# Expert part's first two chunks enter during the last feeding step of an eight-layer linear-attention kernel

## The chip, the cores and the metric

The kernel runs on one core of one Trainium2 chip. The metric is the device time of one execution in microseconds (us), the median over runs. TensorE is called PE here, VectorE DVE, ScalarE ACT, GpSimd POOL, as in the profile. L815 is line 815 of the kernel file.

## The reference, cut to what matters

The input x has 4096 tokens of 128 features. First come eight layers of linear attention with a feed-forward block, each with two layer norms; then a residual layer norm over `x + attention part`; then a mixture of four experts of which each token takes two; then a residual layer norm again.

```python
def _block(x, p):                      # eight times
    Q = elu(x@Wq + bq) + 1; K = elu(x@Wk + bk) + 1; v = x@Wv + bv
    KV = einsum('nsh,nsh->nh', K, v);  Ksum = K.sum(1)
    V = Q * KV / (Q * Ksum + 1e-6)
    x = layernorm(gelu(V@Wo + bo) + x, ln1_s, ln1_b)          # 1e-6
    h = gelu(x@Wf1 + bf1)
    x = layernorm(gelu(h@Wf2 + bf2) + x, ln2_s, ln2_b)
x = _layernorm(x + blocks(x))                                  # 1e-5
h_norm = layer_norm(x, rn_g, rn_b); g = softmax(h_norm @ router_w.T)
top2_w, top2_idx = top_k(g, 2);     top2_w /= top2_w.sum() + 1e-8
hid = relu(layer_norm(einsum('bsd,edh->bseh', x, w1), ln_g, ln_b))
out = sum over the two experts of top2_w * (hid_e @ w2_e)
x = _layernorm(x + layer_norm(out, on_g, on_b))
```

## The kernel before

**Attention part.** The tokens are cut in chunks of 512 columns, features on the partitions. Two chunks (h = 0, 1) are a unit; 4 units times 8 layers make 32 units u = 0 to 31 (`UNITS` = 32). A software pipeline runs over steps s: in step s unit s attends (`attends`), unit s-1 is fed forward (`feeds`), unit s-2 has its second layer norm (`ends`), and s-3 writes the last of it (`closes`). `run` (L321) makes UNITS + 3 steps, so after the last unit has attended in step 31 there come step 32 (unit 31 feeds, unit 30 ends), step 33 (unit 31 ends, the second half of its feed-forward output with it) and step 34 (the last layer norm closes). Each engine has its own list of instructions written out in its own `step` function: the order is by hand, and semaphores tie the lists together. A matrix product in high accuracy is three matmuls (`product`, L681 to L683) on a high and a low part of its operands.

A second layer norm of chunk (u, h) is: `gelu_feed` on ACT (L492), `sum_y`, `high_y`, `low_y` on DVE (L1127, L1134, L1138), `centre` on PE (L799, L800), `square` on ACT (L453), for one half also a cast and a subtraction on DVE (L1145, L1150), `variance` on PE (L818 and L819, or L821), `log_var` and `root` on ACT (L464, L469, as exp(-ln/2)), `normalise` and `high` on DVE (L1160, L1170). GELU and ln/exp need different tables of ACT, loaded by L576 and L619 once each a step.

**Expert part.** Eight chunks. A chunk enters by `add_input` (DVE L1244: last layer's output plus the input x), `turn_z` (PE L867: four transposes so that tokens lie on the partitions), `stats_z` (DVE L1212 to L1232), a power of -1/2 on POOL (`to_minus_half`, L1669), `scale_x` (DVE L1255 to L1264, and POOL L1674), `normalised` (ACT L520, four tiles), `turn_x` (PE L874, back to features on the partitions), `high_x` (ACT L528) and `low_x` (DVE L1270). It is routed by four `gram` products (PE L915 to L917), each followed by `squares` (DVE L1280, four sums), which give the variance of the hidden layer without computing it; then `route` (PE L902 to L904, twelve small matmuls), `gates` (DVE L1316 to L1378), `split_std` (DVE L1291 to L1297), `turn_std` (PE L856) and `rows_of_std` (ACT L507). Then follow `expert_hidden` (PE L888 to L892, eight groups of four) and `expert_out` (PE L925), `mix_tile` (DVE L1392, L1396), and the last norms. A PSUM bank O[0] holds one gram at a time, so a gram waits for the squares of the one before.

`run_moe` (L329) calls the expert steps: in step (0, k) chunk k is routed, chunk k+1 enters, chunk k-1 goes through the experts. Before, chunk 0 enters at the end of step 34 of `run` (the blocks `if s == UNITS + 2`), and the first expert step, `step(0, 0, True, True, False, False)`, routes chunk 0 and lets chunk 1 enter, with no expert work beside it. The table `MIXED`, and `C` and `L` (L173, L325) say which PSUM banks these parts use; `xt_done`, `zt_mm` and `xe_l_done` are the semaphores of `normalised`, `turn_z` and `low_x`.

## Time and profile before

| | |
|---|---|
| median of 3 runs | 1051.41 us (1050.92 to 1051.62) |
| profiled execution | 1052.19 us, its span 1050.1 us |
| mean granted clock of PE | 0.972 |
| busy over the span | PE 961.6 us (92%), DVE 881.4 (84%), ACT 828.6 (79%), POOL 111.5 (11%) |
| instructions | 13399 |

Times in the trace count from the start of the span. The busy time of PE is that of its pipelined matmuls, so a share near 100% is not PE at its peak. The granted clock is a share of PE's 2.4 GHz; 0.50 is 1.2 GHz.

### The profile page before, as it was taken

The page shows a single profiled execution, that of the slowest core. Times are in us where ns is not written, and L with a number is a line of the kernel's source. Part 1 is how long each engine was busy: PE and PEld are TensorE (multiplying, and loading weights), DVE is VectorE, ACT ScalarE, POOL GpSimd, SP SyncE. Part 2 cuts the span into 40 slices and gives each one's busy share as a digit, 9 for nine tenths or more (in the row PEclk, how much of TensorE's full clock was granted, in tenths as well). Part 3 has the DMA queues.
Part 4 walks back from the last instruction along what each step waited for, and adds up shares of the span by engine and source line. Part 5 has one row for each costly group of instructions (what it writes and reads, how often), then busy time and mean ns, then how long its engine had stood idle before and what let it go on. Part 6 is the DMA issues. An engine that isn't in the chain of part 4 may idle for free. (4 is left out here: it accounts for less than half of the span.)

```text
span 1050.1 us, 13399 instructions
## 1 busy us (share of the span) xinstructions
PE 961.6 (92%) x3621; PEld 610.8 (58%) x3621; DVE 881.4 (84%) x2312; ACT 828.6 (79%) x1336; POOL 111.5 (11%) x113
## 2 busy tenths in 40 slices
PE   5799999999999999999999999999998379999993
PEld 3555555555555555655555555555554157877772
DVE  6769999999999999999999999999985457788864
ACT  4689999999999999999899999999987324444452
POOL 3100000000000000000000000000010012323233
PEclk9999999999999999999999999999999669999997
DMA  8000000000000000200000000000020000000000
GB/s 327 1 0 1 1 1 1 0 1 1 1 0 1 1 1 0 81 1 1 1 5 2 1 1 1 1 1 0 1 81 1 0 0 1 12 11 12 11 21 20
DMA packets 8184, 15.86 MB, mean 15 GB/s; under 512 B 944, under 2 KB 5424, under 8 KB 7984
## 3 DMA queue, kind: packets, MB, share of 16 engines
q1 hardware_dynamic: 7680, 14.82, 4.0%
q8 instruction: 31, 0.51, 0.2%
q14 instruction: 41, 0.34, 0.1%
q10 hardware_dynamic: 432, 0.20, 0.1%
HBM read 12.92 MB, written 2.10 MB: 14 GB/s over the span
## 5 line engine op out<-in xcount | busy, mean ns | idle before, releaser
L483 ACT ACTIVATE hid<-R,par 128x512 f32<-128x512 f32 x224 | 148.5, 698 | 15.1 <-PE R L683 13.1
L783 PE MATMUL Oa<-hid,wraw 128*128 128x512 f32 x256 | 133.6, 604 | 1.4
L783 PE MATMUL Ob<-hid,wraw 128*128 128x512 f32 x256 | 130.5, 592 | 0.0
L681 PE MATMUL R<-x_h,wf_h 128*128 128x512 f32 x224 | 105.4, 471 | 0.9 <-ACT hid L483 0.9
L681 PE MATMUL R<-xr_h,wqkv_h 128*128 128x512 f32 x160 | 87.5, 547 | 14.6 <-DVE cen L1512 10.3
L1127 DVE SCALAR_TENSOR_TENSOR y<-x,par,y 128x512 f32<-128x512 f32 x120 | 87.4, 747 | 11.3 <-ACT y L492 11.0
L464 ACT ACTIVATE rs<-SV,eps_ln 128x512 f32<-128x512 f32 x128 | 88.3, 690 | 8.7 <-PE SV L821 6.3
L1138 DVE TENSOR_TENSOR y_l<-y,y_h 128x512 fp32r<-128x512 f32 x128 | 87.8, 686 | 1.2
L682 PE MATMUL R<-x_l,wf_h 128*128 128x512 f32 x224 | 88.0, 393 | 0.0
L683 PE MATMUL R<-x_h,wf_l 128*128 128x512 f32 x224 | 87.9, 392 | 0.0
L469 ACT ACTIVATE rs<-rs 128x512 f32<-128x512 f32 x128 | 80.7, 631 | 1.2
L821 PE MATMUL SV<-y,mean_all 128*128 128x512 f32 x128 | 65.9, 596 | 3.0 <-ACT y L453 2.1
L1114 DVE SCALAR_TENSOR_TENSOR V<-Q,kv,rz 128x512 f32<-128x512 f32 x64 | 46.6, 748 | 24.0 <-ACT rz L448 24.0
L681 PEld LDWEIGHTS R<-x_h,wf_h 128*128 128x128 f32 x224 | 42.0, 187 | 42.0 <-issue 36.0
L783 PEld LDWEIGHTS Oa<-hid,wraw 128*128 128x128 f32 x256 | 45.8, 188 | 35.4 <-ACT hid L483 26.1
L683 PE MATMUL R<-xr_h,wqkv_l 128*128 128x512 f32 x160 | 63.7, 398 | 0.0
L682 PE MATMUL R<-xr_l,wqkv_h 128*128 128x512 f32 x160 | 63.5, 397 | 0.0
L783 PEld LDWEIGHTS Ob<-hid,wraw 128*128 128x128 f32 x256 | 48.3, 189 | 26.2 <-issue 18.2
L681 PEld LDWEIGHTS R<-xr_h,wqkv_h 128*128 128x128 f32 x160 | 30.5, 191 | 54.8 <-DVE xr_l L1183 27.8
L1134 DVE CAST y_h<-y 128x512 fp32r<-128x512 f32 x128 | 54.4, 425 | 9.0 <-PE R L800 6.8
L554 ACT ACTIVATE reluq<-V,rz 128x128 f32<-128x128 f32 x32 | 13.2, 482 | 60.4 <-DVE rz L1411 44.5
L453 ACT ACTIVATE y<-Ca 128x512 f32<-128x512 f32 x64 | 38.0, 595 | 27.3 <-PE Ca L800 27.2
(215 smaller groups left out, 2448.5 us busy)
## 6 DMA issues: line engine op xcount, KB each, us to landing
wraw<-w_dram SPq DMA_DIRECT2D x7, 768.0 KB, 12.1
x<-x_dram SPq DMA_DIRECT2D x8, 256.0 KB, 5.5
Q<-x_dram SPq DMA_DIRECT2D x1, 2048.0 KB, 7.5
out_dram<-reluq SPq DMA_DIRECT2D x8, 256.0 KB, 2.3
wraw<-w_dram SPq DMA_DIRECT2D x2, 512.0 KB, 4.9
wraw<-w_dram SPq DMA_DIRECT2D x1, 576.0 KB, 5.7
wraw<-row_dram SPq DMA_DIRECT2D x1, 512.0 KB, 4.4
wraw<-bias_dram SPq DMA_DIRECT2D x1, 512.0 KB, 5.6
```

The costliest lines, as they stand in the source:

```text
L464: nc.scalar.activation(rs[:, half(h)], SV[:, :], ACT.Ln, bias=eps_ln[:, :]).then_inc(ln_done[which], 1)
L469: nc.scalar.activation(rs[:, half(h)], rs[:, half(h)], ACT.Exp, scale=-0.5).then_inc(rs_done[which], 1)
L483: nc.scalar.activation(hid[:, m * CH:(m + 1) * CH], HIDDEN[m][:, :], GELU, bias=param(u // 4, BF1 + m % FB)).then_inc(hid_done, 1)
L681: nc.tensor.matmul(bank, w_h, a_h, start=True, stop=False)
L682: nc.tensor.matmul(bank, w_h, a_l, start=False, stop=False)
L683: return nc.tensor.matmul(bank, w_l, a_h, start=False, stop=True)
L783: mm = nc.tensor.matmul(O[h][:, :], raw(u // 4, WF2 + j * P, P), hid[:, m * CH:(m + 1) * CH], start=(j == 0), stop=(j == FB - 1))
L821: mm = nc.tensor.matmul(SV[:, :], mean_all[:, :], y[which][:, half(h)], start=True, stop=True)
L1114: nc.vector.scalar_tensor_tensor(out=V[:, half(h)], in0=Q[:, chunk(u, h)], scalar=kv[:, b:b + 1], in1=rz[:, half(h)], op0=ALU.mult, op1=AL ...
L1127: nc.vector.scalar_tensor_tensor(out=g, in0=t, scalar=b, in1=g, op0=ALU.add, op1=ALU.add).then_inc(y_done[which], 1)
L1134: nc.vector.tensor_copy(y_h[:, half(h)], y[which][:, half(h)]).then_inc(yh_done[which], 1)
L1138: nc.vector.tensor_tensor(y_l[:, half(h)], y[which][:, half(h)], y_h[:, half(h)].bitcast(F32), ALU.subtract).then_inc(yl_done[which], 1)
```

## The change

It runs steps 0 to 32 of `run` and drops steps 33 and 34. Into step 32 go: the entering of chunk 0 and of chunk 1 (with `turn_z`, `stats_z`, `scale_x`, `normalised`, `turn_x`, `high_x`, `low_x` of both), and the rest of unit 31's feed-forward output (`feed_out` 4 to 7, `gelu_feed(31, 1)`, `sum_y`, `high_y`, `low_y` of its second half). A new function `last_layer_norms` on each of PE, ACT and DVE takes the place of steps 33 and 34 and of `step(0, 0)`: the last three chunk norms (30, 1), (31, 0), (31, 1) with the four grams and squares of expert chunk 0 between them, then its route, gates and `turn_std`. POOL keeps its `step(0, 0)` as a call of its own. For this the banks of the expert part are exchanged (`C` is CB[1], `L` has CB[0]), the centred values of (31, 1) go to R[1], and some waits name other semaphores.

```diff
-        C, L = CB[0], (SV, CB[1])
+        C, L = CB[1], (SV, CB[0])
...
+        def centred(which, u, h):
+            return R[1] if (which, u, h) == (1, UNITS - 1, 1) else CENTRED[which][h]
...
-            for s in range(UNITS + 3):
+            for s in range(UNITS + 1):
...
         def run_moe(step):
-            step(0, 0, True, True, False, False)
...
+            def last_layer_norms():                     (ACT)
+                u = UNITS - 1
+                nc.scalar.preload_act_table_set("natural_log_exp_and_others")
+                log_var(1, u - 1, 1)
+                root(1, u - 1, 1)
+                square(1, u, 0)
+                square(1, u, 1)
+                log_var(1, u, 0)
+                root(1, u, 0)
+                log_var(1, u, 1)
+                root(1, u, 1)
+                roots_of_hidden(0, 0)
+                exp_logits(0, 0)
+                rows_of_std(0, 0)
...
-                    pe.wait_ge(norm_done[1], 2 * UNITS)     (turn_z, first chunk)
+                    pe.wait_ge(norm_done[0], 2 * UNITS)
...
+                if s == UNITS:                          (PE, step 32, after feed_out 3)
+                    turn_z(0, 1)
                 if ends:
                     variance(1, s - 2, 1)
+                if s == UNITS:
+                    feed_out(s - 1, 4)
+                    feed_out(s - 1, 5)
+                    feed_out(s - 1, 6)
+                    feed_out(s - 1, 7)
+                    turn_x(0, 1)
...
+            def last_layer_norms():                     (PE)
+                u = UNITS - 1
+                gram(0, 0, 0)
+                centre(1, u, 0)
+                gram(0, 0, 1)
+                variance(1, u, 0)
+                centre(1, u, 1)
+                gram(0, 0, 2)
+                variance(1, u, 1)
+                gram(0, 0, 3)
+                route(0, 0)
+                turn_std(0, 0)
...
+            def last_layer_norms():                     (DVE)
+                u = UNITS - 1
+                weave(squares(0, 0, 0))
+                normalise(1, u - 1, 1)
+                high(1, u - 1, 1)
+                weave(squares(0, 0, 1))
+                high_square(1, u, 1)
+                low_square(1, u, 1)
+                weave(squares(0, 0, 2))
+                normalise(1, u, 0)
+                high(1, u, 0)
+                weave(squares(0, 0, 3))
+                normalise(1, u, 1)
+                high(1, u, 1)
+                gating = gates(0, 0)
+                weave(itertools.islice(gating, 7))
+                split_std(0, 0)
+                weave(gating)
```

The words in brackets are mine. How the instructions move is seen at three places. Oa, Ob, Ca, Cb and SV are PSUM banks; every line number is that of the kernel file shown, so the same function has another number in the changed file.

**PE, from the last variance of step 32 on.** Before (L818 to L821 are variances, L783 a feed-forward output, L799 and L800 a centring, L867 `turn_z`):

```order
L818 MATMUL SV<-sq_h,mean_r 128x512
L819 MATMUL SV<-sq_l,mean_r 128x512
L783 MATMUL Ob<-hid,wraw 128x512 x3
L799 MATMUL Ca<-y_h,cen 128x512
L800 MATMUL Ca<-y_l,cen 128x512
L821 MATMUL SV<-y,mean_all 128x512
L783 MATMUL Ob<-hid,wraw 128x512
L799 MATMUL R<-y_h,cen 128x512
L800 MATMUL R<-y_l,cen 128x512
L818 MATMUL SV<-sq_h,mean_r 128x512
L819 MATMUL SV<-sq_l,mean_r 128x512
L867 MATMUL Ca<-consts,y 128x128 x4
```

In the changed kernel (L897 is `turn_z`, L904 `turn_x`, L848, L849 and L851 variances, L813 a feed-forward output, L829 and L830 a centring, L951 to L953 a gram):

```order
L897 MATMUL Cb<-consts,y 128x128 x4
L848 MATMUL SV<-sq_h,mean_r 128x512
L849 MATMUL SV<-sq_l,mean_r 128x512
L813 MATMUL Ob<-hid,wraw 128x512 x4
L904 MATMUL Cb<-consts,x 128x128 x4
L951 MATMUL Oa<-xr_h,x_h 128x512
L952 MATMUL Oa<-xr_h,x_l 128x512
L953 MATMUL Oa<-xr_l,x_h 128x512
L829 MATMUL Ca<-y_h,cen 128x512
L830 MATMUL Ca<-y_l,cen 128x512
L951 MATMUL Oa<-xr_h,x_h 128x512
L952 MATMUL Oa<-xr_h,x_l 128x512
```

The four feed-forward outputs are now in one row, the transposes of chunk 1 stand around them, and the centring of unit 31's first half stands between two grams of chunk 0.

**ACT, from the last GELU of step 32's hidden layer on.** Before (L483 `gelu_hidden`, L492 `gelu_feed`, L464 and L469 the root of the variance, L453 `square`, L520 `normalised`, L528 `high_x`):

```order
L483 ACTIVATE hid<-R,par 128x512
L492 ACTIVATE y<-Oa,par 128x512
L576 ACT_TABLE_LOAD
L464 ACTIVATE rs<-SV,eps_ln 128x512
L469 ACTIVATE rs<-rs 128x512
L453 ACTIVATE y<-Ca 128x512
L464 ACTIVATE rs<-SV,eps_ln 128x512
L469 ACTIVATE rs<-rs 128x512
L619 ACT_TABLE_LOAD
L492 ACTIVATE y<-Ob,par 128x512
L453 ACTIVATE y<-R 128x512
L576 ACT_TABLE_LOAD
```

In the changed kernel, from four GELUs earlier on (L487, L496, L468, L457, L524 and L534 are the same functions):

```order
L487 ACTIVATE hid<-R,par 128x512 x4
L524 ACTIVATE x<-Cb,rz 128x128 x4
L487 ACTIVATE hid<-R,par 128x512 x2
L534 ACTIVATE x_h<-Cb 128x512
L457 ACTIVATE y<-R 128x512
L487 ACTIVATE hid<-R,par 128x512
L496 ACTIVATE y<-Oa,par 128x512
L496 ACTIVATE y<-Ob,par 128x512
L524 ACTIVATE x<-Cb,rz 128x128 x4
L534 ACTIVATE x_h<-Cb 128x512
L669 ACT_TABLE_LOAD
L468 ACTIVATE rs<-SV,eps_ln 128x512
```

Both entries of a chunk (L524, L534) and both `gelu_feed` (L496) now stand under one table. From the first `gelu_feed` on, one table load is left in the layer norms (L669), where there were three (L576, L619, L576).

**DVE in the changed kernel, step 32, behind the statistics of chunk 0.** L1306 is `add_input` of chunk 1, L1189 `sum_y`, L1196 `high_y`, L1222 `normalise`, L1200 `low_y`, and L1317 begins `scale_x` of chunk 0:

```order
L1294 TENSOR_SCALAR rz<-rz 128x4
L1306 TENSOR_TENSOR y<-x,Q 128x512
L1189 SCALAR_TENSOR_TENSOR y<-x,par,y 128x512
L1196 CAST y_h<-y 128x512
L1222 SCALAR_TENSOR_TENSOR x<-Ca,par,rs 128x512
L1200 TENSOR_TENSOR y_l<-y,y_h 128x512
L1317 SCALAR_TENSOR_TENSOR rz<-rz 128x4
L1320 TENSOR_TENSOR rz<-rz 128x4
```

The mean that `normalised` needs (from L1317 on) stands behind four instructions of unit 30's layer norm; before, nothing stood between it and the statistics.

## Rows read from the trace of the kernel before

**Rows 1.** Windows: busy us per engine in a stretch, count in brackets, then PEclk, DMA share, GB/s.

```profile
42.00:44.00 2.00, 2.00 (x5) 1.61 (x6) 1.30 (x2) 1.31 (x3) 0.00 (x0) 0.50 0.03 8
820.00:855.00 35.00, 15.67 (x44) 9.93 (x44) 15.99 (x84) 8.17 (x18) 5.28 (x5) 0.50 0.00 0
855.00:861.00 6.00, 5.94 (x18) 4.59 (x19) 4.27 (x23) 1.36 (x3) 0.00 (x0) 0.50 0.00 0
880.00:1020.00 140.00, 129.64 (x798) 107.91 (x797) 109.87 (x664) 63.70 (x154) 45.89 (x41) 1.00 0.04 11
```

**Rows 2.** PE's timeline, norms to experts: start us, us, instruction, count, [idle before <-releaser].

```profile
815.61 1.02 PE L783 MATMUL Ob<-hid,wraw 128*128 128x512 f32 x2
...
821.72 0.80 PE L799 MATMUL R<-y_h,cen 128*128 128x512 f32 x1 [5.09 <-DVE y_l L1138]
...
829.46 1.11 PE L867 MATMUL Ca<-consts,y 128*128 128x128 f32 x4 [3.35 <-DVE y L1244]
835.45 1.12 PE L874 MATMUL Ca<-consts,x 128*128 128x128 f32 x4 [4.88 <-ACT x L520]
838.07 0.76 PE L915 MATMUL Oa<-xr_h,x_h 128*128 128x512 f32 x1 [1.50 <-DVE x_l L1270]
...
847.49 0.77 PE L915 MATMUL Oa<-xr_h,x_h 128*128 128x512 f32 x1 [1.74 <-DVE Kt L1280]
...
850.23 0.34 PE L902 MATMUL Oa<-rw_h,x_h 128*128 128x4 f32 x1 [1.12 <-DVE Kt L1280]
...
855.06 1.04 PE L856 MATMUL SV<-consts,wraw 128*36 128x128 f32 x4 [1.17 <-DVE wraw L1297]
```

**Rows 3.** ACT's timeline, feeding step 32 to the entry of chunk 0.

```profile
806.93 1.38 ACT L483 ACTIVATE hid<-R,par 128x512 f32<-128x512 f32 x2 [0.88 <-PE R L683]
...
817.18 1.28 ACT L619 ACT_TABLE_LOAD   x1
818.48 0.69 ACT L492 ACTIVATE y<-Ob,par 128x512 f32<-128x512 f32 x1
...
833.89 1.50 ACT L520 ACTIVATE x<-Ca,rz 128x128 f32<-128x128 f32 x4 [6.39 <-DVE rz L1255]
836.60 0.60 ACT L528 ACTIVATE x_h<-Ca 128x512 fp32r<-128x512 f32 x1 [1.21 <-PE Ca L874]
```

**Rows 4.** PE and DVE timelines at full clock: one gram round, route, second `turn_std`.

```profile
868.07 0.47 PE L915 MATMUL Oa<-xr_h,x_h 128*128 128x512 f32 x1 [0.62 <-DVE Kt L1280]
...
869.04 0.29 DVE L1280 SCALAR_TENSOR_TENSOR Kt<-Oa,x 128x128 f32<-128x128 f32 x1 [1.12 <-PE Oa L917]
...
870.12 0.24 PE L902 MATMUL Oa<-rw_h,x_h 128*128 128x4 f32 x1 [0.21 <-DVE Kt L1280]
...
871.45 0.66 PE L874 MATMUL Ca<-consts,x 128*128 128x128 f32 x4
...
873.73 0.61 PE L856 MATMUL SV<-consts,wraw 128*36 128x128 f32 x4
```

**Rows 5.** DVE's timeline of the same norms: `sum_y`, `normalise` and `high`.

```profile
819.19 0.75 DVE L1127 SCALAR_TENSOR_TENSOR y<-x,par,y 128x512 f32<-128x512 f32 x1 [4.04 <-ACT y L492]
...
827.53 0.75 DVE L1160 SCALAR_TENSOR_TENSOR x<-R,par,rs 128x512 f32<-128x512 f32 x1 [2.30 <-ACT rs L469]
828.31 0.49 DVE L1170 TENSOR_SCALAR x<-x,par 128x512 f32<-128x512 f32 x1
```

**Rows 6.** PE's timeline, two other idle times: clock kept after one, lost after the other.

```profile
40.57 0.50 PE L799 MATMUL Ca<-y_h,cen 128*128 128x512 f32 x1 [2.57 <-DVE y_l L1138]
...
793.34 0.47 PE L818 MATMUL SV<-sq_h,mean_r 128*128 128x512 f32 x1 [1.54 <-ACT rs L464]
```

**Rows 7.** DVE and POOL timelines: a DVE instruction beside POOL, and `add_on_b` of chunk 0.

```profile
772.36 2.96 DVE L1183 SCALAR_TENSOR_TENSOR x_l<-x,par,x_h 128x512 fp32r<-128x512 f32 x1
...
772.41 2.37 POOL L1635 TENSOR_TENSOR xr_l<-wraw,xr_h 128x1024 fp32r<-128x1024 f32 x1 [21.43 <-DVE x_h L1176]
...
848.20 1.27 POOL L1690 TENSOR_TENSOR expk<-x,wraw 128x512 f32<-128x512 f32 x1
```

More of the change, by code:

```diff
@@ L452, in square @@
                 act.wait_ge(centre_mm[which], upto(u, h))
-                nc.scalar.activation(y[which][:, half(h)], CENTRED[which][h][:, :],
+                nc.scalar.activation(y[which][:, half(h)], centred(which, u, h)[:, :],
                                      ACT.Square).then_inc(sq_done[which], 1)
@@ L614, in step @@
                     exp_z(s)
-                if s == UNITS + 2:
-                    normalised(0, 0)
-                    high_x(0, 0)
-                if s < UNITS + 2:
-                    nc.scalar.preload_act_table_set("gelu_apprx_tanh_and_others")
+                nc.scalar.preload_act_table_set("gelu_apprx_tanh_and_others")
                 if feeds:
@@ L632, in step @@
                     gelu_hidden(s - 1, 4)
+                if s == UNITS:
+                    normalised(0, 0)
+                if feeds:
                     gelu_hidden(s - 1, 5)
                     gelu_hidden(s - 1, 6)
+                if s == UNITS:
+                    high_x(0, 0)
                 if ends:
@@ L645, in step @@
                     gelu_feed(s - 1, 0)
+                if s == UNITS:
+                    gelu_feed(s - 1, 1)
+                    normalised(0, 1)
+                    high_x(0, 1)
             for u in range(2):
@@ L883, in expert_hidden @@
                     pe.wait_ge(relu_done, last + m - 2)
+                elif n > 1:
+                    pe.wait_ge(relu_done, last + (-1, 0, -2)[m])
+                elif m == 0:
+                    pe.wait_ge(hid_done, hid_upto(UNITS - 1, 6))
                 else:
-                    after(pe, relu_done, last + (-1, 0, -2)[m])
+                    pe.wait_ge(norm_done[1], upto(UNITS - 1, 1))
                 w = tile(m)
@@ L910, in gram @@
                 pe.wait_ge(xe_l_done, n)
-                if t == 0:
+                if t == 0 and n == 1:
+                    pe.wait_ge(gelu_done[1], upto(UNITS - 1, 0))
+                elif t == 0:
                     after(pe, gate_step, (n - 2) * GATE_STEPS + 1)
@@ L968, in step @@
                     hidden(s - 1, 1, p)
+                if s == UNITS:
+                    turn_z(0, 0)
+                if feeds:
                     hidden(s - 1, 2, p)
                     hidden(s - 1, 3, p)
-                if s == UNITS + 2:
-                    turn_z(0, 0)
-                    turn_x(0, 0)
                 if s == 0:
@@ L986, in step @@
                     hidden(s - 1, 6, p)
+                if s == UNITS:
+                    turn_x(0, 0)
                 if ends:
@@ L1159, in normalise @@
                 dve.wait_ge(rs_done[which], upto(u, h))
-                nc.vector.scalar_tensor_tensor(out=t, in0=CENTRED[which][h][:, :], scalar=param(u // 4, (S1, S2)[which]),
+                nc.vector.scalar_tensor_tensor(out=t, in0=centred(which, u, h)[:, :], scalar=param(u // 4, (S1, S2)[which]),
                                                in1=rs[:, half(h)], op0=ALU.mult,
@@ L1447, in step @@
                     low(0, s - 1, 0)
+                if s == UNITS:
+                    add_input(0, 0)
                 if s == UNITS - 1:
@@ L1466, in step @@
                     low(0, s - 1, 1)
+                if s == UNITS:
+                    weave(stats_z(0, 0))
+                    add_input(0, 1)
                 if ends:
@@ L1471, in step @@
                     low_y(1, s - 2, 1)
+                if s == UNITS:
+                    weave(scale_x(0, 0))
                 if attends:
@@ L1489, in step @@
                     high(1, s - 2, 0)
+                if s == UNITS:
+                    low_x(0, 0)
+                    weave(stats_z(0, 1))
+                if ends:
                     low(1, s - 2, 0)
@@ L1497, in step @@
                     low_y(1, s - 1, 0)
-                if s == UNITS + 2:
-                    add_input(0, 0)
-                    weave(stats_z(0, 0))
-                    weave(scale_x(0, 0))
-                    low_x(0, 0)
+                if s == UNITS:
+                    weave(scale_x(0, 1))
+                    sum_y(1, s - 1, 1)
+                    high_y(1, s - 1, 1)
+                    low_y(1, s - 1, 1)
+                    low_x(0, 1)
             split_qkv_first()
@@ L1710, in step @@
                     to_minus_half(2, it, k - 2)
+            step(0, 0, True, True, False, False)
             run_moe(step)
```

23 lines of the change are left out of this document (18 added, 5 removed).

## The prediction

> **What bounds the kernel now.** I read the windows first. From 880 to 1020 us, in the expert steps, PE is busy 129.64 of 140 us at clock 1.00 [rows 1]: PE bounds that part, and the change leaves it alone. From 820 to 855 us it is busy 15.67 of 35 us, and its clock is at 0.50 (1.2 GHz) [rows 1]. No engine is full there: DVE is busy 15.99 us and ACT 8.17 [rows 1]. That stretch is a chain of waits, and the timeline of PE shows its links. The last feed-forward output ends at 815.61 + 1.02 = 816.63; the next matmul, the last centring, starts at 821.72 after 5.09 us of idle time; the transposes of chunk 0 wait 3.35 us for its `add_input` at 829.46 and 4.88 us for the normalised tiles at 835.45; its first gram starts at 838.07, its route at 850.23, its `turn_std` at 855.06 [rows 2]. From 816.63 to 855.06 are 38.43 us in which one chunk's norm, entry and routing go one after the other. A gram round costs 850.23 - 847.49 = 2.74 us there, with PE idle 1.74 us before a gram [rows 2]. After `turn_std` PE is busy 5.94 of 6 us, and still at clock 0.50 [rows 1]; later it is at 1.00.
>
> **The change, part by part.** I follow the path to the first `turn_std`, in five parts.
>
> *A, longer step 32.* Before its last outputs step 32 now does the entry of chunk 0. On ACT four `normalised` (1.50) and one `high_x` (0.60) are put among the GELUs of the hidden layer [rows 3]. They are 2.10 us in an in-order list; before the GELUs at 806.93 ACT was idle 0.88 us [rows 3], which takes up part. That leaves 2.10 - 0.88 = **+1.22 us**. PE's added sets of transposes are short at full clock (0.61 to 0.66 us a set, [rows 4]) and lie in its waits for ACT and DVE. If that cover were gone, three sets (two `turn_z`, one `turn_x`) would add up to 1.9 us, some 3.1 in all; the other end is 0, if ACT's idle time takes everything. I take 1.22, since PE waits for ACT there. The last output then ends at 817.85. DVE's statistics, its sums for the mean and POOL's power move too; they end before ACT's entry work can begin, in the time of unit 30's last norms, and I cost them at nothing.
>
> *Beside A, POOL against DVE.* With chunk 0 entered early, its `add_on_b` on POOL (1.27 us, [rows 7]) comes while DVE does the sums of the last norm, as `sum_y`, which took 0.75 us [rows 5]. At 772.36 a DVE instruction of the same size took 2.96 us, beside a POOL instruction of 2.37 us [rows 7]. So the price lies between 0 and 1.27 us. I take 0.2: there is slack after `sum_y`, as the first gram waits for chunk 1's entry on ACT, not for unit 31's sums. The Trainium skill ("SBUF - State Buffer", section "SBUF: two separate sides") speaks against the change here: the loser of the shared port pair waits for the other's whole instruction. The 2.96 us agrees with it; by that rule the full 1.27 us could be paid.
>
> *B, to the first gram.* Before, ACT loaded a table for 1.28 us between the last output and `gelu_feed` at 818.48 [rows 3]; now the GELU table is still there. Behind it stand `normalised` and `high_x` of chunk 1, then DVE's `low_x`, and PE's list has `turn_x(0, 1)` ahead of the first gram. From `normalised` at 833.89 to the gram at 838.07 are 4.18 us [rows 2, 3] with transposes of 1.12 us at half clock, against 0.66 at full [rows 2, 4], so 3.72. Add 0.69 for `gelu_feed`: **4.4 us**, first gram at 822.25.
>
> The Trainium skill ("ScalarE: Activation LUTs", section "What ACT_TABLE_LOAD costs") adds a drain of about 1.38 us to each switch. The trace does not: the load starts at 817.18 and the GELU at 818.48, 1.30 us later [rows 3]. By the page the removed load would give an estimated 1.4 us more; I count none.
>
> *C, four gram rounds.* At full clock a round takes 870.12 - 868.07 = 2.05 us [rows 4], four of them 8.20. Into DVE's wait for each gram (1.12 us, [rows 4]) go a `normalise` and a `high`, 0.75 + 0.49 = 1.24 us [rows 5]: 0.12 us too long, three times. PE's centrings and variances go beside the squares. Together **8.6 us**; route at 830.85. All three norms, and the table load for them, are hidden here: their cover is PE and DVE alternating on Oa.
>
> *D, route to `turn_std`.* 873.73 - 870.12 = **3.61 us** at full clock [rows 4], against 855.06 - 850.23 = 4.83 at half [rows 2]. Nothing is left to lie beside it. With the 0.2 of POOL, `turn_std` comes at 834.65 instead of 855.06: **-20.4 us**.
>
> *E, what comes behind.* Before, 5.94 us of PE's work after `turn_std` ran at half clock [rows 1]. At full it would take half, 2.97 us; I take **-2.7**, as DVE's squares hold a gram for a part. With a full clock the sum is -23.1 us.
>
> **The clock.** Whether it holds is the largest unknown. In B PE has nothing but `turn_x` for 4.4 us, in D it waits 2 us. The clock stayed at 1.00 after an idle time of 1.54 us, and after one of 2.57 us it fell [rows 6], standing at 0.50 from 42 to 44 us though PE was busy 2.00 of 2.00 us [rows 1]. The idle times of B, some 2.3 and 1.4 us with the transposes between, are nearer to the second. Half clock costs in C four times 2.74 - 2.05 = 0.69, less the 0.36 that then fits in DVE's longer waits, 2.4 us; in D 1.22; in E the 2.7: 6.3 us together. But in C PE now has the grams, two centrings and two variances, so it is busier than from 820 to 855 us, and after steady work the clock rose before. I take the clock to fall in B and to come back on the way, at half of that price, 3.15 us.
>
> The traced execution took 1052.19 us, 0.78 above the median of 1051.41, which is what runs are compared by; the difference is taken as the same. Sum of the forecast: 1051.41 - 23.1 + 3.15 = **1031.5 us**.
>
> **The rivals.**
>
> 1. *The clock holds.* No 3.15: 1028.3 us. For it: 1.54 us of idle time did no harm [rows 6]. Against: 2.57 us did.
> 2. *Half clock from B into E.* All 6.3 us: 1034.6 us. For it: PE at 0.45 busy never got the clock back from 820 to 855 us [rows 1].
> 3. *The entry isn't hidden.* The engines' lists are in order, and DVE's has chunk 0's mean behind four instructions of unit 30's norm, which waits for its GELU. If these waits lock the two chains to each other, one entry, from 829.46 to 838.07 = 8.61 us [rows 2], comes back onto the path: 1040.1 us. Against it: step 32 has the same GELUs and outputs to do meanwhile.
> 4. *Slower: the clock does not come back.* It falls in B and stays at half in the expert steps, because PE's first expert work stands behind waits for norms that end later than I think. Those steps are 0.926 busy at full clock [rows 1], so at half each of their microseconds takes up to 1.85. The gain, some 17 us at half clock, is used up after 17 / 0.85 = 20 us of them; two times that long gives about 1051 + 17 = 1068 us. Against it: after `turn_std` the changed kernel has the same dense expert work.
> 5. *It does not do what it says.* A semaphore that now comes later holds the new steps to the old order, and nothing moves: 1051.4 us.
>
> **How the numbers follow.** Forecast 0.50, rival 1 0.21, rival 2 0.20, rival 3 0.06, rival 4 0.02, rival 5 0.01. The range starts at rival 1 with A at its lower end, 1028.3 - 1.2 = 1027.1, and ends at rival 2 with A at its upper end, 1034.6 + 1.9 = 1036.5; that leaves out rivals 3 to 5 and little else. A measurement of this kernel can tell about 0.2% (2.1 us) from no change. All but rivals 4 and 5 are faster by more: faster 0.97, same 0.01, slower 0.02.
>
> **What would show it.** In the changed profile: the four feed-forward outputs end near 817.9 (A); the first gram at 822.3 (B), with PE idle twice in front of it; gram starts 2.1 to 2.7 us apart (C); route to `turn_std` 3.6 to 4.8 us, `turn_std` between 834.6 and 838.3 (D); clock 0.50 from about 821 us in windows of a microsecond, and 1.00 again before or soon after `turn_std`. `sum_y(31, 1)` well above 0.75 us would be POOL's price. I am wrong if `turn_std` comes after 842 (then a wait in step 32 or in C is the reason, and the row before the late gram names it), or if the expert steps are no longer some 0.93 busy at clock 1.00.

## The result, and the profile after

The changed kernel takes **1032.42 us** (median of 4 runs, 1032.17 to 1032.62) against 1051.33 (4 runs): a ratio of 0.982, 95% interval 0.9806 to 0.9834. That is 18.9 us less; 1031.5 was forecast, in a range of 1027.1 to 1036.5. On a second chip, beside its own runs of the kernel before, it was again 19.0 us under it (1032.47 against 1051.49). The profiled execution took 1032.47 us with a span of 1029.0, so 3.5 us lie outside its span, and 2.1 us before the change; its three other runs have spans of 1030.1 to 1030.6. Spans therefore flatter the change by about 1.4 us, and times are compared by medians below.

| | before | after |
|---|---|---|
| profiled span | 1050.1 us | 1029.0 us |
| mean granted clock | 0.972 | 0.987 |
| last feed-forward output ends | 816.63 | 817.06 |
| first gram | 838.07 | 819.64 |
| route | 850.23 | 830.89 |
| first `turn_std` | 855.06 | 835.35 |
| second `turn_std` | 873.73 | 852.61 |

PE's timeline of the changed kernel, beside [rows 2] (L813 is a feed-forward output, L897 `turn_z`, L904 `turn_x`, L951 a gram, L829 a centring, L851 and L848 variances, L936 the route, L886 `turn_std`):

```profile
808.04 0.66 PE L904 MATMUL Cb<-consts,x 128*128 128x128 f32 x4 [0.94 <-ACT x L524]
...
812.52 0.63 PE L897 MATMUL Cb<-consts,y 128*128 128x128 f32 x4 [0.94 <-DVE x_l L1332]
...
813.46 3.60 PE L813 MATMUL Ob<-hid,wraw 128*128 128x512 f32 x8
819.23 0.65 PE L904 MATMUL Cb<-consts,x 128*128 128x128 f32 x4 [2.17 <-ACT x L524]
819.64 0.47 PE L951 MATMUL Oa<-xr_h,x_h 128*128 128x512 f32 x1
...
822.39 0.47 PE L951 MATMUL Oa<-xr_h,x_h 128*128 128x512 f32 x1 [1.34 <-DVE Kt L1342]
...
823.72 1.38 PE L851 MATMUL SV<-y,mean_all 128*128 128x512 f32 x2 [0.39 <-ACT y L457]
824.28 1.24 PE L829 MATMUL R<-y_h,cen 128*128 128x512 f32 x1
...
825.75 0.63 PE L951 MATMUL Oa<-xr_h,x_h 128*128 128x512 f32 x1
...
827.90 0.50 PE L848 MATMUL SV<-sq_h,mean_r 128*128 128x512 f32 x1 [0.66 <-DVE sq_l L1212]
...
828.84 0.47 PE L951 MATMUL Oa<-xr_h,x_h 128*128 128x512 f32 x1 [0.20 <-DVE Kt L1342]
...
830.89 0.24 PE L936 MATMUL Oa<-rw_h,x_h 128*128 128x4 f32 x1 [1.11 <-DVE Kt L1342]
...
835.35 1.04 PE L886 MATMUL SV<-consts,wraw 128*36 128x128 f32 x4 [2.14 <-DVE wraw L1359]
```

The 5.09, 3.35 and 4.88 us of idle time of [rows 2] are gone; 2.17 and 2.14 us are the longest left. The first gram follows the last output by 2.58 us. The four grams lie 2.75, 3.36 and 3.09 us apart, and the third waits for no square: it stands behind a variance and a centring in PE's own list.

DVE's timeline of the same stretch (L1189 `sum_y`, L1196 `high_y`, L1200 `low_y`, L1332 `low_x` of chunk 1, L1342 the squares, L1222 `normalise` of (30, 1), L1207 the cast of the square of (31, 1)) and POOL's (L1785 is `add_on_b` of chunk 0):

```profile
817.82 0.75 DVE L1189 SCALAR_TENSOR_TENSOR y<-x,par,y 128x512 f32<-128x512 f32 x1 [0.34 <-ACT y L496]
818.60 1.48 DVE L1196 CAST y_h<-y 128x512 fp32r<-128x512 f32 x1
820.11 0.69 DVE L1200 TENSOR_TENSOR y_l<-y,y_h 128x512 fp32r<-128x512 f32 x1
820.72 0.68 DVE L1332 TENSOR_TENSOR x_l<-Cb,x_h 128x512 fp32r<-128x512 f32 x1
821.32 0.28 DVE L1342 SCALAR_TENSOR_TENSOR Kt<-Oa,x 128x128 f32<-128x128 f32 x1
...
823.22 0.75 DVE L1222 SCALAR_TENSOR_TENSOR x<-R,par,rs 128x512 f32<-128x512 f32 x1 [0.98 <-ACT rs L473]
...
826.62 0.43 DVE L1207 CAST sq_h<-y 128x512 fp32r<-128x512 f32 x1 [1.29 <-ACT y L457]
```

```profile
818.53 1.26 POOL L1785 TENSOR_TENSOR expk<-x,wraw 128x512 f32<-128x512 f32 x1
```

The cast at 818.60 takes 1.48 us beside POOL; the one of unit 31's first half took 0.43. `sum_y` itself, which the forecast had named, takes 0.75 as before.

Windows of the changed kernel (the columns of [rows 1]):

```profile
820.00:824.00 4.00, 2.27 (x9) 1.28 (x8) 2.96 (x12) 3.61 (x5) 0.00 (x0) 1.00 0.00 0
824.30:827.90 3.60, 2.94 (x7) 1.44 (x6) 2.21 (x12) 1.80 (x3) 0.00 (x0) 0.53 0.00 0
828.00:831.20 3.20, 1.89 (x8) 1.03 (x9) 3.17 (x19) 1.72 (x4) 0.00 (x0) 1.00 0.00 0
831.40:838.00 6.60, 4.46 (x18) 3.78 (x19) 4.44 (x25) 0.84 (x3) 0.00 (x0) 0.50 0.00 0
838.00:858.00 20.00, 19.21 (x124) 16.38 (x123) 12.48 (x81) 7.98 (x18) 2.03 (x2) 1.00 0.00 1
```

The clock fell twice and came back twice. Before, it stood at 0.50 from 820 to 861 us [rows 1]; now for 3.6 and for 6.6 us, and the expert work gets it back at 838.

### The profile page after: what moved, and what is told of

Same layout as the page of the kernel before. It is cut to its first block and busy times, and to the rows that moved or that the text cites. A ratio compares the mean times of both kernels' runs of the same rounds, so it can differ in the third digit from the quotient of the medians.

```text
span 1029.0 us, 13409 instructions
## 1 busy us (share of the span) xinstructions
PE 954.8 (93%) x3621; PEld 607.2 (59%) x3621; DVE 881.8 (86%) x2312; ACT 825.3 (80%) x1334; POOL 112.3 (11%) x113
## 5 line engine op out<-in xcount | busy, mean ns | idle before, releaser
L487 ACT ACTIVATE hid<-R,par 128x512 f32<-128x512 f32 x224 | 148.5, 698 | 14.2 <-PE R L713 12.2
L813 PE MATMUL Oa<-hid,wraw 128*128 128x512 f32 x256 | 133.6, 604 | 1.5
L813 PE MATMUL Ob<-hid,wraw 128*128 128x512 f32 x256 | 130.3, 592 | 0.0
L711 PE MATMUL R<-xr_h,wqkv_h 128*128 128x512 f32 x160 | 87.5, 547 | 14.1 <-DVE cen L1586 10.2
L468 ACT ACTIVATE rs<-SV,eps_ln 128x512 f32<-128x512 f32 x128 | 88.3, 690 | 7.2 <-PE SV L851 5.1
L1189 DVE SCALAR_TENSOR_TENSOR y<-x,par,y 128x512 f32<-128x512 f32 x120 | 87.4, 747 | 4.3 <-ACT y L496 4.0
L1200 DVE TENSOR_TENSOR y_l<-y,y_h 128x512 fp32r<-128x512 f32 x128 | 87.7, 685 | 1.2
L851 PE MATMUL SV<-y,mean_all 128*128 128x512 f32 x128 | 66.1, 598 | 2.5 <-ACT y L457 1.8
L813 PEld LDWEIGHTS Oa<-hid,wraw 128*128 128x128 f32 x256 | 45.9, 188 | 35.3 <-ACT hid L487 25.9
L813 PEld LDWEIGHTS Ob<-hid,wraw 128*128 128x128 f32 x256 | 48.3, 189 | 26.2 <-issue 18.2
L1196 DVE CAST y_h<-y 128x512 fp32r<-128x512 f32 x128 | 55.5, 434 | 9.0 <-PE R L830 6.8
L562 ACT ACTIVATE reluq<-V,rz 128x128 f32<-128x128 f32 x32 | 13.2, 482 | 60.4 <-DVE rz L1473 44.6
L457 ACT ACTIVATE y<-Ca 128x512 f32<-128x512 f32 x64 | 38.0, 594 | 27.2 <-PE Ca L830 27.2
```

Source lines behind the costliest of these rows:

```text
L468: nc.scalar.activation(rs[:, half(h)], SV[:, :], ACT.Ln, bias=eps_ln[:, :]).then_inc(ln_done[which], 1)
L487: nc.scalar.activation(hid[:, m * CH:(m + 1) * CH], HIDDEN[m][:, :], GELU, bias=param(u // 4, BF1 + m % FB)).then_inc(hid_done, 1)
L711: nc.tensor.matmul(bank, w_h, a_h, start=True, stop=False)
L813: mm = nc.tensor.matmul(O[h][:, :], raw(u // 4, WF2 + j * P, P), hid[:, m * CH:(m + 1) * CH], start=(j == 0), stop=(j == FB - 1))
L851: mm = nc.tensor.matmul(SV[:, :], mean_all[:, :], y[which][:, half(h)], start=True, stop=True)
L1189: nc.vector.scalar_tensor_tensor(out=g, in0=t, scalar=b, in1=g, op0=ALU.add, op1=ALU.add).then_inc(y_done[which], 1)
```

## The experiments

Each time is compared with the kernel before on the same chip. Positions in different traces are compared from F, the start of the row of the last four feed-forward outputs (813.46 us in the changed kernel), because F itself differs by up to 1.3 us from trace to trace. One reason seen in the traces is PE's clock further ahead: near 40 us it falls for 3 to 7 us, in one trace not at all, and in two traces it falls near 771 us as well. The changed kernel's `turn_std` comes at F + 21.89 and F + 39.15.

**Keep the clock.** In the changed kernel, `keep_busy(n)` issues n matmuls into a bank that nobody reads then:

```diff
+            def keep_busy(n):
+                for _ in range(n):
+                    nc.tensor.matmul(R[0][:, :], cen[:, :], gram_h, start=True, stop=True)
...
                     feed_out(s - 1, 7)
+                    keep_busy(8)
                     turn_x(0, 1)
...
                 centre(1, u, 0)
+                keep_busy(4)
                 gram(0, 0, 1)
+                keep_busy(1)
...
                 gram(0, 0, 2)
+                keep_busy(2)
...
                 gram(0, 0, 3)
+                keep_busy(3)
                 route(0, 0)
+                keep_busy(8)
                 turn_std(0, 0)
```

> The changed kernel with matmuls of no use on PE (bank R[0], which nobody reads then) put into its idle times: 8 before turn_x(0, 1), 4 behind the first centring, 1, 2 and 3 behind grams 1, 2 and 3, 8 behind the route. They are meant to keep the clock, and they fit into the idle times at full clock. Theory A (the half clock from about 824 to 828 and from 831 to 838 us costs time): the clock stays at 1.00, turn_std comes some 1 us earlier than in the changed kernel, the second turn_std 2.3 us earlier, and the time falls by 2.0 to 2.5 us. Rival (the path in this stage is DVE's and ACT's, and PE's clock is hidden): the clock stays, but the time changes by less than 0.7 us. If the clock falls in spite of them, they lie in PE's way and the time rises by 0.5 to 1 us.

Measured: 1029.39 us against 1052.21 (ratio 0.9766 to 0.9798), 22.8 us less, where the changed kernel has 18.9. Its window, and its timeline of PE with the first gram, the route and both `turn_std`:

```profile
814.00:850.00 36.00, 32.92 (x149) 22.74 (x147) 26.21 (x136) 17.04 (x35) 5.72 (x5) 1.00 0.00 1
```

```profile
820.84 0.47 PE L955 MATMUL Oa<-xr_h,x_h 128*128 128x512 f32 x1
...
831.44 0.24 PE L940 MATMUL Oa<-rw_h,x_h 128*128 128x4 f32 x1 [0.41 <-DVE Kt L1352]
...
835.06 0.61 PE L890 MATMUL SV<-consts,wraw 128*36 128x128 f32 x4 [0.19 <-DVE wraw L1369]
...
851.28 0.61 PE L890 MATMUL SV<-consts,wraw 128*36 128x128 f32 x4
```

The clock stays at 1.00, and 26 matmuls of no use cost nothing: the first gram is at F + 6.19 (F + 6.18 in the changed kernel). F is at 814.65, so `turn_std` is at F + 20.41 and F + 36.63: 1.48 and 2.52 us earlier. By the trace the two falls of the clock cost 2.5 us, 1.5 of it ahead of `turn_std`. The medians give 3.9, each against its own chip's kernel before, 1.4 us more than this stage shows; where that lies isn't shown. Theory A's mechanism holds, with more than the 2.0 to 2.5 us that it expected by the medians.

**POOL beside `high_y`.**

```diff
+                    if it == 0 and k == 1:
+                        pool.wait_ge(relu_done, 2)
                     add_on_b(it, k - 1)
```

> The changed kernel with POOL's add_on_b of chunk 0 held back until two relu of the first expert step are done, so that it does not run beside DVE's high_y(31, 1) at 818.6 us. Theory A (the 1.48 us of that cast, 0.43 elsewhere, are POOL's work beside it, and the delay lies on the path): high_y takes 0.43 us, the first squares start when the gram is done, up to 0.7 us earlier, and the time falls by 0.4 to 0.7 us. Rival (the delay is caught by waits behind it): high_y takes 0.43 us and the time changes by less than 0.3 us. Second rival (the long cast has another cause): it stays at 1.4 us or more.

Measured: 1031.99 us against 1052.21 (0.9794 to 0.9823), 20.2 us less. DVE's timeline:

```profile
819.29 0.43 DVE L1196 CAST y_h<-y 128x512 fp32r<-128x512 f32 x1
819.75 0.69 DVE L1200 TENSOR_TENSOR y_l<-y,y_h 128x512 fp32r<-128x512 f32 x1
821.24 0.69 DVE L1332 TENSOR_TENSOR x_l<-Cb,x_h 128x512 fp32r<-128x512 f32 x1 [0.80 <-ACT x_h L534]
821.85 0.28 DVE L1342 SCALAR_TENSOR_TENSOR Kt<-Oa,x 128x128 f32<-128x128 f32 x1
```

The cast takes 0.43 us again, so the 1.05 us were POOL's work beside it. But DVE now waits 0.80 us for `high_x` at `low_x`, and the squares start at F + 7.70 (F is 814.15) instead of F + 7.86. A wait took the place of the one removed. By the medians the gain is 1.3 us larger all the same, but the intervals overlap. In this execution the clock fell once, in the window below, and not twice: the first `turn_std` (834.55) is at F + 20.40, 1.49 us earlier, the second (853.08) at F + 38.93, only 0.22 us earlier. So most of the 1.3 us isn't in this stage.

```profile
833.00:840.00 7.00, 5.45 (x15) 4.15 (x16) 4.75 (x29) 1.41 (x3) 0.00 (x0) 0.52 0.00 0
```

To take the clock out, both edits were made together.

> The kernel with PE's idle times filled (as in the first experiment) and POOL's add_on_b held back (as in the second): with the clock steady the price of POOL beside high_y can be read alone. Theory A (that price is hidden: in the second experiment DVE waited 0.80 us for high_x where the long cast had been, and the squares came only 0.16 us earlier): 0.1 to 0.3 us under the first experiment, both against their kernels before. Rival (the 1.2 us that the second experiment lay under the changed kernel are POOL's price): 0.8 us or more under the first experiment.

Measured: 1028.63 us against 1052.27 (0.9761 to 0.9796), 23.6 us less. Its `turn_std` are at 833.79 and 850.01 with F at 813.39: F + 20.40 and F + 36.62, within 0.01 us of the experiment without the POOL edit. So POOL's price in this stage is nothing. The 0.8 us between the medians meet the words of the rival, but the intervals overlap, and the traces show a difference ahead of the stage: F comes 1.26 us earlier here. The clock was at 0.50 from 771 to 774.8 us in the trace without the POOL edit, and at 1.00 there in this one. The Trainium skill ("SBUF - State Buffer", section "SBUF: two separate sides") names the cause of a long cast beside POOL, and the 1.48 us agree with it; whether it costs anything was a question of what comes next in DVE's list.

**Undo the interleaving.** On PE `centre`, `variance`, `centre`, `variance`, and then four grams; on DVE the norms' instructions, and then four rounds of squares. The early entry stays. The second text below is the same order with 51 matmuls of no use in PE's idle times.

```diff
-                gram(0, 0, 0)
                 centre(1, u, 0)
-                gram(0, 0, 1)
                 variance(1, u, 0)
                 centre(1, u, 1)
-                gram(0, 0, 2)
                 variance(1, u, 1)
+                gram(0, 0, 0)
+                gram(0, 0, 1)
+                gram(0, 0, 2)
                 gram(0, 0, 3)
```

> The changed kernel with the interleaving undone on PE and DVE: the last three layer norms run first and the four grams with their squares behind them; everything enters early as in the changed kernel. Theory A (both parts are worth something): turn_std comes 7 to 9 us later than in the changed kernel, the time is 7.5 to 8.5 us longer, about 1040.5 us, so the early entry alone is worth some 11 us and the interleaving some 8. Rival (the early entry does it all, since the norms' chain is the bound either way): less than 3 us longer. Other rival (it is the interleaving that does it): more than 14 us longer.

> The third experiment's kernel (norms first, then the four grams) with PE's idle times filled by matmuls of no use. It tells how much of the interleaving's 10 us is order and how much is the clock, which stood at 0.50 from 823 us to the first expert step there and for shorter stretches in the changed kernel. Theory A (order is worth about 7.5 us, the clock the rest): the time is 7 to 8 us over the first experiment's (the interleaved kernel with the clock kept), so 15 us under the kernel before. Rival (the wait chain is PE's at half clock in both, and order alone is worth 4 us or less): 18 us or more under the kernel before. The clock stays at 1.00 in either.

Measured: 1043.54 us against 1052.21 (0.9904 to 0.9933), only 8.7 us less; with the idle times filled 1037.05 against 1052.27 (0.984 to 0.9875), 15.2 us less. Windows of the first, and then the first `turn_std` of the first and of the second:

```profile
814.00:822.70 8.70, 5.33 (x19) 2.54 (x17) 7.55 (x22) 3.69 (x7) 3.68 (x3) 0.98 0.00 1
823.00:853.00 30.00, 18.29 (x45) 11.94 (x46) 13.71 (x71) 6.94 (x14) 0.00 (x0) 0.50 0.00 0
```

```profile
847.69 1.04 PE L886 MATMUL SV<-consts,wraw 128*36 128x128 f32 x4 [2.14 <-DVE wraw L1359]
```

```profile
841.91 0.61 PE L890 MATMUL SV<-consts,wraw 128*36 128x128 f32 x4 [0.17 <-DVE wraw L1371]
```

That is F + 33.08 (F is 814.61) and F + 27.96 (F is 813.95). At full clock the interleaving is worth 27.96 - 20.41 = 7.55 us, as the second text expected. The first text missed: it had 7.5 to 8.5 us and some 11 for the early entry, and the medians gave 10.2 and 8.7, since it had not counted the clock. The clock at 0.50 for 30 us costs the kernel with the norms first 6.5 us by the medians (7.4 by the traces, at the second `turn_std`), where it costs the interleaved kernel 3.9 by the medians (2.5 by the traces). So the interleaving gives twice: it saves 7.5 us of waits, and the kernel loses less clock. By the medians, 8.7 of the 18.9 us are then the early entry and the merged step with all their loss of clock, 7.5 the order, and the 2.7 that are left the clock that the order saves.

**The root of (30, 1) early, with two more table loads.**

```diff
                     gelu_feed(s - 1, 0)
+                    nc.scalar.preload_act_table_set("natural_log_exp_and_others")
+                    log_var(1, s - 2, 1)
+                    root(1, s - 2, 1)
+                    nc.scalar.preload_act_table_set("gelu_apprx_tanh_and_others")
                     gelu_feed(s - 1, 1)
```

> The changed kernel with ACT's log_var and root of (30, 1) done in its idle time of 4.8 us behind gelu_feed(31, 0), with two more table loads (ln/exp, then GELU again), so that DVE does not wait 0.98 us for that root between the first two rounds of squares. Theory A (the wait for the root is on the path of the rounds, and table loads in idle time cost nothing): DVE's wait is gone, turn_std comes 1.0 to 1.6 us earlier, and the time falls by 0.9 to 1.2 us. Rival (a table switch costs more than the 1.28 us of its row, or the second gram round is held by something else): the time stays within 0.3 us or rises, with gelu_feed(31, 1) later than 817.1 us.

Measured: 1032.29 us against 1052.21 (0.9792 to 0.9821), 19.9 us less. ACT's timeline, and two rows of DVE's:

```profile
813.16 1.28 ACT L656 ACT_TABLE_LOAD   x1
814.48 0.69 ACT L468 ACTIVATE rs<-SV,eps_ln 128x512 f32<-128x512 f32 x1
815.20 0.63 ACT L473 ACTIVATE rs<-rs 128x512 f32<-128x512 f32 x1
815.85 1.28 ACT L659 ACT_TABLE_LOAD   x1
817.91 0.69 ACT L496 ACTIVATE y<-Ob,par 128x512 f32<-128x512 f32 x1 [0.78 <-PE Ob L815]
```

```profile
823.33 0.75 DVE L1224 SCALAR_TENSOR_TENSOR x<-R,par,rs 128x512 f32<-128x512 f32 x1
...
826.50 0.43 DVE L1209 CAST sq_h<-y 128x512 fp32r<-128x512 f32 x1 [1.02 <-ACT y L457]
```

The table loads cost nothing, `gelu_feed(31, 1)` keeps its place (F + 3.63, in the changed kernel F + 3.64), and DVE's wait for the root is gone. But DVE still waits 1.02 us for ACT's square of (31, 1), where it waited 1.29, and `turn_std` is at F + 21.32, 0.57 us earlier, the second at F + 39.50, 0.35 us later, in an execution whose clock fell from 820 to 823.5 and again from 830.6 to 840.8 us. Measured against the changed kernel the 1 us is within the intervals. That the wait goes and that the loads cost nothing is shown; the gain that theory A expected is not.

**The changed kernel again, and chunk 1 taken out of step 32.**

```diff
-                    turn_z(0, 1)
-                    turn_x(0, 1)
...
                 gram(0, 0, 0)
+                turn_z(0, 1)
...
                 route(0, 0)
+                turn_x(0, 1)
```

with `stats_z` beside the second squares, `scale_x` beside the fourth, `normalised` behind the last root, `high_x` behind `exp_logits` and `low_x` behind `split_std`.

> The changed kernel itself once more, on the chip of the next two, so that they are compared with it and not with another chip's run. Expected from its first runs: 18.9 us under the kernel before, within 0.5 us; the clock falls somewhere between 820 and 834 us, not at the same instant as in the first trace.

> The changed kernel with the entry of chunk 1 taken out of step 32 again (all but its add_input): turn_z(0, 1) behind the first gram, its statistics and scale beside the second and fourth squares, normalised behind the last root, turn_x behind the route, high_x and low_x before rows_of_std and the late gates, as the first expert step had it. Theory A (DVE is the engine that sets the pace between 813 and 831 us, where chunk 1's entry puts 3.3 us of DVE work and 2.1 us of ACT work ahead of chunk 0's squares, and the stage has idle time for it later): turn_std comes 2 to 3 us earlier than in the changed kernel and the time falls by 1.5 to 2.5 us. Rival (chunk 1's early entry is part of the gain, as the change has it): the time rises by 1 us or more. Null: within 0.5 us.

Measured: 1032.47 us for the changed kernel (0.98 to 0.9836) and 1030.12 for the other (0.9775 to 0.981), both against 1051.49. In the second trace of the changed kernel the clock is at 0.50 from 821.0 to 824.7 and from 831.6 to 841.2 us; the first of the two:

```profile
821.00:824.70 3.70, 3.37 (x10) 2.09 (x8) 2.66 (x12) 3.40 (x5) 0.07 (x1) 0.54 0.00 0
```

Without chunk 1's early entry the time is 2.35 us *less*; the intervals overlap a little, but the slowest of its four runs (1030.58) is faster than the fastest of the changed kernel's (1031.71). The first feed-forward output stands elsewhere now, so the traces are counted from a matmul of the hidden layer, at 805.25 (803.93 in the first trace of the changed kernel, 805.21 in the second): `turn_std` at 833.65 is 3.0 us earlier than in the first and 2.8 than in the second, and the second `turn_std` at 852.11 is 1.8 and 2.6 us earlier. Its clock was at 0.50 for some 14 us, as in the second trace of the changed kernel and longer than in the first (10), so the gain isn't the clock's. DVE's timeline shows what became free, a wait of 2.06 us for the last GELU where chunk 1's work had been:

```profile
814.48 0.43 DVE L1195 CAST y_h<-y 128x512 fp32r<-128x512 f32 x1
814.94 0.69 DVE L1199 TENSOR_TENSOR y_l<-y,y_h 128x512 fp32r<-128x512 f32 x1
817.70 0.75 DVE L1188 SCALAR_TENSOR_TENSOR y<-x,par,y 128x512 f32<-128x512 f32 x1 [2.06 <-ACT y L496]
```

So this part of the change works against it: it puts chunk 1's work ahead of chunk 0's on an engine that the stage waits for. Theory A holds.

**Chunk 0's grams among the feed-forward outputs.** PE's order, with the norms' indices as (unit, half), from the hidden layer on:

```diff
-turn_x(0,0) centre(30,1) hidden 7, feed_out 2, 3, turn_z(0,1) variance(30,1) feed_out 4, 5, 6, 7,
-turn_x(0,1) gram 0, centre(31,0) gram 1, variance(31,0) centre(31,1) gram 2, variance(31,1) gram 3,
-route, turn_std
+centre(30,1) turn_x(0,0) hidden 7, feed_out 2, turn_z(0,1) feed_out 3, 4, 5, gram 0, feed_out 6, 7,
+gram 1, variance(30,1) gram 2, centre(31,0) centre(31,1) gram 3, turn_x(0,1) variance(31,0) route,
+variance(31,1) turn_std
```

DVE has the squares right behind their grams, and `high` of the last norms inside or behind the gates; chunk 1's `normalised` and `high_x` on ACT stand behind the root of (30, 1), its `low_x` on DVE behind the last squares; ACT has `log_var` and `root` of (30, 1) behind `gelu_feed(31, 1)`, as the changed kernel has.

> Another order of the same instructions from the hidden layer's GELU 5 of step 32 to turn_std, on PE, ACT and DVE, with add_on_b held back as in the experiment on it: chunk 0's grams go between the last feed-forward outputs (the first behind output 5), their squares between the sums of the last two norms; the root of (30, 1) is in ACT's idle time with two more table loads; the route stands ahead of the last variance; chunk 1's transposes back and its high_x, low_x come behind the fourth gram. Theory A (the grams need only chunk 0, which is in place at 812.4 us, and nothing but their place in the lists keeps them until 819.6): turn_std comes 7 to 8 us earlier than in the changed kernel at the same clock and the time falls by 5.5 to 7 us, to about 1026. Rival (the work moved behind turn_std delays the first expert step by as much): turn_std earlier, but the second turn_std within 2 us of the changed kernel's, and the time falls by less than 2 us. Second rival (the clock falls in the earlier, thinner stretch and eats it): the gain is 3 us or less with the clock at 0.50 for more than 10 us.

That text is wrong in one point: the kernel has no more table loads than the changed one; its only one follows `gelu_feed(31, 1)`. Measured: **1022.86 us** against 1051.49 (0.971 to 0.9741), 28.6 us less, and in a later repeat 1023.22 against 1051.20 (0.9718 to 0.9744), 28.0 less. It beats both kernels. PE's rows, and windows from the output row to `turn_std`, first of the changed kernel, then of this one:

```profile
813.72 0.79 PE L954 MATMUL Oa<-xr_h,x_h 128*128 128x512 f32 x1
...
827.20 1.04 PE L889 MATMUL SV<-consts,wraw 128*36 128x128 f32 x4 [1.72 <-DVE wraw L1364]
...
844.79 0.61 PE L889 MATMUL SV<-consts,wraw 128*36 128x128 f32 x4
```

```profile
813.46:835.35 21.89, 13.86 (x45) 7.89 (x43) 16.91 (x73) 9.74 (x19) 3.68 (x3) 0.83 0.00 0
```

```profile
812.41:827.20 14.79, 11.54 (x47) 7.03 (x45) 14.02 (x69) 10.10 (x20) 2.45 (x2) 0.98 0.00 1
827.00:831.00 4.00, 3.80 (x13) 3.01 (x14) 3.69 (x17) 1.28 (x3) 0.00 (x0) 0.61 0.00 0
```

The first gram ran at 813.72 instead of 819.64, between the outputs; it was its place in PE's list that had kept it. But grams and squares are not all that moved: chunk 1's turn back stands behind chunk 0's grams too, as in the experiment before, so the 9.6 us hold some of those 2.35 and the two don't add up. DVE is busy 14.02 of 14.79 us (95%), against 16.91 of 21.89 (77%): now DVE is close to full. The gain is larger than expected (9.6 us against 5.5 to 7). The clock was at 0.50 for 3.4 us here and for 10 to 14 in the changed kernel; the next experiment tells how much of the gain that is.

> The kernel with chunk 0's grams among the last feed-forward outputs, with 4 matmuls of no use in PE's idle time of 1.34 us before the third gram and 6 in the 1.72 us before turn_std. Theory A (its clock at 0.50 from 827 to 831 us, over the start of the first expert step, costs 2 us or more, as it did in the changed kernel): the clock stays at 1.00, turn_std within 0.2 us, the second turn_std 2.0 to 2.5 us earlier, and the time falls by 2 to 2.5 us, to about 1020.7 us. Rival (the expert step has slack at half clock): less than 1 us. If the clock falls all the same, the time is within 0.5 us.

Measured: 1022.82 us against 1052.27 (0.9705 to 0.9735), 29.4 us less. From the row of feed-forward outputs 4 and 5 (812.41 and 811.86 us), `turn_std` comes 14.79 us later in both, and the second 32.38 and 32.36 us later. The clock stays at 1.00 and gives nothing: the rival. With the first experiment there are now both orders with the clock kept. Counted from the same matmul of the hidden layer (805.14 there, 804.14 here), the first `turn_std` comes after 29.92 and 22.51 us, the second after 46.14 and 40.08: the order alone gives 7.4 and 6.1 us. The medians say 29.4 - 22.8 = 6.6, inside the 5.5 to 7 that were expected, and by the medians some 3 of the 9.6 us are the clock. PE's timeline of the filled kernel's first expert step shows a wait in it:

```profile
831.21 0.66 PE L904 MATMUL Cb<-consts,y 128*128 128x128 f32 x4 [1.15 <-DVE y L1317]
```

`turn_z` waits for chunk 2's `add_input`, which stands behind the gates in DVE's list.

> As the kernel with the grams among the last feed-forward outputs, no added matmuls, in a further order of the same instructions: chunk 0's first gram behind output 4, the second behind 6, its third behind output 7 and the variance of (30, 1), the routing ahead of more of unit 31's norm work, and chunk 2's add_input, which stood behind all the gates at the head of the next expert step, already in step 32. Theory A (in that kernel's first expert step turn_z waits for this add_input, 1.15 us in the trace with the clock kept, and the step has 1.35 us more between its turn_std than the changed kernel's): the two turn_std come 16.2 to 16.8 us apart at full clock instead of 17.6, and the time is 1 to 1.5 us under the next run's. Rival (the clock, or DVE beside it, takes it back): within 0.4 us of it.

> The kernel with the grams among the last feed-forward outputs once more, as the partner of the run before on the same chip. Expected: 28.6 us under the kernel before, within 0.5 us.

Measured: 1022.33 (0.971 to 0.9737) and 1023.22 us, both against 1051.20: 0.9 us apart, less than the intervals tell. The two `turn_std` of the first, 825.82 and 843.36, are 17.54 us apart, but its clock was at 0.50 from about 826.4 to 829.7 us, so 16.2 to 16.8 at full clock was neither met nor refuted. The partner lies 28.0 us under the kernel before, where 28.1 to 29.1 was expected.

## Why the prediction was right

The time, 1032.42, lies 0.9 us over the forecast of 1031.5, and the mechanism was the one forecast: one merged stage in place of a chain, with the clock lost on the way and back again. That it is as near as 0.9 us is in part luck. B and C were wrong in opposite directions, and A is a net of two parts of which the forecast had one. A row of the kernel before for A, outputs 4 to 6 of unit 31:

```profile
810.76 2.73 PE L783 MATMUL Ob<-hid,wraw 128*128 128x512 f32 x6
```

- **A, longer step 32**: +1.22 forecast. From the variance at 793.34 [rows 6] (792.85 after) the last output came 23.29 us later before and 24.21 after: +0.92. The number is near, the account isn't. Output 4 starts 17.42 us after that variance before and 20.61 after: the entry of chunk 0, with two waits of 0.94 us at `turn_x(0, 0)` and `turn_z(0, 1)`, costs 3.2 us there, as much as the upper end of A, and the second wait is for DVE's `low_x`, not for ACT. From the start of output 4 to the end of the last it took 5.87 us before, with a centring and a variance in between, and takes 3.60 now: 2.3 us come back, which the forecast did not have.
- **B, to the first gram**: 4.4 forecast, 2.58 measured. The step "behind it stand `normalised` and `high_x` of chunk 1, then DVE's `low_x`" failed: gram (0, 0, 0) reads chunk 0 alone. Only `turn_x(0, 1)`, which stands ahead of it in PE's list, held it, so `high_x` and `low_x` of chunk 1 did not count. I had priced the other chunk's chain.
- **C, four rounds**: 8.6 forecast, 830.89 - 819.64 = 11.25 measured. With the clock kept it is 831.44 - 820.84 = 10.60, so order, and not clock, made most of it. The step "All three norms, and the table load for them, are hidden here" failed. Into DVE's waits I had put one `normalise` and one `high` a round and nothing else. There are also the last sums and chunk 1's `low_x` ahead of the first squares, a wait of 0.98 us for a root that stands behind the table load, a cast and a subtraction ahead of the third squares with a wait of 1.29 us for ACT's square, and on PE a variance and a centring that hold the third gram. B's error and the full-clock part of C's nearly cancel: 13.0 forecast, 13.2 measured.
- **D, route to `turn_std`**: 3.61 at full clock; 4.46 measured, and 835.06 - 831.44 = 3.62 with the clock kept. Right; the 4.46 lie between its two ends, 3.61 and 4.83, with the clock falling at 831.4.
- **E**: 2.7 at full clock. The two `turn_std` are 17.26 us apart against 18.67: 1.4 less. With the clock kept they are 16.22 apart: 2.45 less. Right in size, slightly high.
- **The clock**: 3.15 us for a fall in B and a return on the way. It fell twice and came back twice, the first time in C and not in B (at 824.3 us in this trace, 821.0 in the other of the same kernel), and PE was idle once and not twice ahead of the first gram. By the filled kernel's trace it costs 2.5 us: 0.65 in C, 0.84 in D, 1.04 in E, where the forecast had half of 2.4, 1.22 and 2.7. The full-clock sum was -23.1 us; the filled kernel is 22.8 us under its kernel before. Rival 1 (1028.3) is near what the kernel is with its clock kept (1029.4), and rival 2 did not come true, since the clock was back for C's end.
- **POOL beside DVE**: 0.2 taken of 0 to 1.27. The effect is there, in `high_y` (1.48 instead of 0.43) and not in `sum_y` (0.75), the cost is not: 0.01 us. The slack I named was the wrong one, though: the wait behind it was DVE's for `high_x` of chunk 1.
- **Rival 3**, the entry not hidden, did not come true: of its 8.61 us, the 3.2 of A are what the entry costs on the path.
- **The table load**: two loads added in idle time moved nothing, and `log_var` followed the first one's start by 1.32 us. The drain of about 1.38 us a switch that the Trainium skill states ("ScalarE: Activation LUTs", section "What ACT_TABLE_LOAD costs") did not show there.

What I did not see at all is that chunk 1's early entry costs 2.35 us, and that another order of the stage, with the grams further ahead and chunk 1's turn back behind them, gives 9.6 in all, some 6.6 of it by the order alone. Both follow from one question that I did not ask of the list: which of these instructions does the next `turn_std` need?

## What to carry to other kernels

When engines run lists in order, ask of each item ahead of a long chain whether that chain needs it; the work that was moved early "to have it done" stood in front of the chain here and cost 2.35 us, and an order with the chain's own first steps among dense work, and the other work behind them, was 9.6 us faster. Before pricing a wait in such a chain, follow the semaphores of the instruction itself and then its place in the list, separately. And where PE idles in short pieces, fill the idle time once with matmuls of no use: here it cost nothing, showed what the clock is worth (3.9 us by the medians in one order, nothing in another), and made traces comparable.

## What the runs showed of the hardware that I had not expected

- The clock does not fall at the same instant in two executions of the same kernel: from 824.3 to 827.9 and from 831.4 to 838 us in one, from 821.0 to 824.7 and from 831.6 to 841.2 in the other. The longest idle time of PE ahead of the first fall was 2.17 us in one and 2.18 in the other, and with `add_on_b` held back the same 2.17 us brought no fall until 833.3 us. In those two traces of one kernel the second `turn_std` is 48.7 and 49.5 us behind the same matmul, a difference of 0.8 us.
- In a chain of waits the clock can stay low for long: 30 us at 0.50 where the norms came first, with PE busy 18.29 of them, and 6.5 us of time.
- At half clock a stretch may cost nothing: 4 us at 0.61 at the start of the first expert step were hidden behind DVE.
- DVE's cast of 0.43 us took 1.48 us beside a POOL instruction of 1.26 us, and POOL's own small power took 1.43 us at 803.37 us, beside DVE's large instructions, where it took 1.02 before. The small power at 815.17 took 1.44 us and did not hold DVE's cast at 815.78, which took 0.43.
